# Expert tiles in three groups, half A combined beside the last experts, and one-hot rows made eight choices at a time

## The reference

```python
def _L0_ffn_ref(hidden_states, gate_w, gate_up_proj, down_proj):   # 16 experts, top 2
    logits = x @ gate_w.T
    p = sigmoid(logits); p = p / sum(p)
    w, idx = top_k(p, 2)
    w = w / sum(w)
    gu = einsum('th,ehf->etf', x, gate_up_proj)
    gate, up = split(gu, 2)
    y = einsum('eti,eih->eth', silu(gate) * up, down_proj)
    out = einsum('eth,te->th', y, combine)
x = x + 0.5 * ffn(layernorm(x))
x = x + attn(layernorm(x))          # 16 heads of 16, causal softmax
x = x + 0.5 * ffn(layernorm(x))
```

## Time and profile before

| | us |
|---|---|
| time, median of 3 runs | 887.43 (885.02 to 888.61) |
| profiled execution | 886.32 |
| its span, first to last instruction | 884.6 |
| TensorE busy | 662.1 (75%) |
| VectorE busy | 574.8 (65%) |
| GpSimd busy | 395.4 (45%) |
| ScalarE busy | 366.6 (41%) |
| TensorE's share of the chain that ended last | 64% |

### The profile page before, as it was taken

One profiled execution on the slowest core, in us unless ns is written; L12 is line 12 of the kernel. 1 busy time (PEld: TensorE's weight loads), 2 busy tenths in 40 slices (PEclk: granted clock), 3 DMA queues, 4 the chain that ended last, 5 costly groups with the idle time before them and its releaser, 6 DMA issues.

```text
span 884.6 us, 17856 instructions
## 1 busy us (share of the span) xinstructions
PE 662.1 (75%) x5016; PEld 507.6 (57%) x5017; DVE 574.8 (65%) x1599; ACT 366.6 (41%) x941; POOL 395.4 (45%) x467
## 2 busy tenths in 40 slices
PE   2614999999078999999999999866159999990000
PEld 2402888887056777777777777544038888870000
DVE  6597455555758888878888877646964555553333
ACT  2417334444025555555656655454263333430000
POOL 4101655553453554444555422240026555536775
PEclk9955999999678999999999999988559999995555
DMA  7680455557263444444444433014004555574554
GB/s 238 219 258 10 142 162 162 160 160 137 65 185 106 132 128 120 121 116 129 114 109 121 113 107 97 4 48 144 0 24 142 162 162 161 161 130 130 153 152 142
DMA packets 94136, 113.36 MB, mean 128 GB/s; under 512 B 11633, under 2 KB 84609, under 8 KB 94081
## 3 DMA queue, kind: packets, MB, share of 16 engines
q1 hardware_dynamic: 80224, 74.87, 27.5%
q0 software_dynamic: 13824, 37.77, 17.5%
q10 hardware_dynamic: 32, 0.02, 0.0%
HBM read 49.30 MB, written 33.55 MB: 94 GB/s over the span
## 4 chain that ended last, share of the span: by engine, by line
PE 64%; DVE 12%; DMA 8%; issue 5%; POOL 5%; ACT 4%; SPq 1%; DVEq 0%; ACTq 0%; POOLq 0%
PE bank L774 16%; PE bank L785 8%; PE bank L352 6%; PE bank L411 5%; PE bank L372 5%; PE bank L397 5%; PE bank L767 4%; POOL shared L649 4%; DMA shared<-grouped_out,slot 3%; PE bank L359 3%; PE bank L375 3%; PE bank L431 3%; PE bank L780 2%; DMA normed<-shared 2%; ACT shared L885 1%
## 5 line engine op out<-in xcount | busy, mean ns | idle before, releaser
L632 POOL DMA_INDIRECT shared<-normed,source x160 | 152.3, 952 | 213.4 <-DVE source L1043 111.2
L774 PE MATMUL bank<-wgu_sb,xeT 128*128 x640 | 167.8, 386 | 0.0
L306 POOL TENSOR_SCALAR_AFFINE_SELECT pr<-pr 128x512 f32<-128x512 f32 x128 | 81.0, 655 | 154.8 <-ACT pr L476 154.6
L534 DVE TENSOR_REDUCE mx<-bank 128x2 f32<-128x512 f32 (+1 forms) x192 | 127.0, 685 | 23.6 <-PE bank L375 20.4
L1053 DVE COPY hidT<-bank 128x128 f32<-128x128 f32 x160 | 46.6, 291 | 116.8 <-PE bank L780 115.9
L774 PEld LDWEIGHTS bank<-wgu_sb,xeT 128*128 128x128 f32 x640 | 111.5, 194 | 8.8
L476 ACT ACTIVATE pr<-bank 128x512 f32<-128x512 f32 x192 | 102.9, 609 | 30.6 <-PE bank L397 18.1
L785 PE MATMUL bank<-wd_sb,hidT 128*128 x320 | 95.6, 382 | 0.0
L868 ACT COPY xeT<-bank 128x256 f32<-128x256 f32 x160 | 59.5, 372 | 84.6 <-PE bank L767 84.3
L294 POOL DMA_INDIRECT gathered_rows<-grouped_out,slot x64 | 69.0, 1078 | 27.8 <-DMA grouped_out<-shared 13.4
L872 ACT ACTIVATE silu<-bank 128x128 f32<-128x128 f32 x160 | 44.4, 278 | 83.2 <-PE bank L774 83.2
(11 more groups left out here) (148 smaller groups left out, 1118.2 us busy)
## 6 DMA issues: line engine op xcount, KB each, us to landing
grouped_out<-shared SPq DMA_DIRECT2D x160, 128.0 KB, 1.7
shared<-parts SPq DMA_DIRECT2D x154, 128.0 KB
spare<-parts SPq DMA_DIRECT2D x70, 128.0 KB
normed<-shared SPq DMA_DIRECT2D x16, 512.0 KB, 3.1
x_sb<-in_L_attn_x_dram SPq DMA_DIRECT2D x4, 1024.0 KB, 9.7
wgu_sb<-_L_ffn_gate_up_proj_dram SPq DMA_DIRECT2D x8, 512.0 KB, 8.6
out_dram<-x_sb SPq DMA_DIRECT2D x16, 256.0 KB, 2.6
shared<-normed,source POOLq DMA_INDIRECT x160, 2.8
```

The lines of the kernel that those rows point to most:

```text
L306: nc.gpsimd.affine_select(out=m, in_=m, compare_op=ALU.is_ge, fill=0.0, base=0, pattern=[[0, 4], [1, P]], channel_multiplier=-1).then_inc( ...
L534: nc.vector.tensor_reduce(mx[:, u, h0:h0 + nh], bank[3 + n % 2][:, :].rearrange("p (h k) -> p h k", h=nh), AX.X, ALU.max).then_inc(at["max ...
L632: nc.gpsimd.indirect_dma_start(xe[:, r, :], None, normed, bass.IndirectOffsetOnAxis(source[:, j:j + 1], 0)).then_inc(s["xe_loaded"][r], 16)
L774: last = nc.tensor.matmul(bank[2 + u][:, 0:2 * I], xeT[:, u, c, :], wgu_sb[:, e, c, :], start=(c == 0), stop=(c == HC - 1))
```

## The change

**Expert tiles in three groups.** The 32 token tiles are two halves, A (the first 16) and B. The expert tiles are now laid out as: full tiles that hold only half A's choices (for each expert as many as its count in half A fills), then one tile for each of the 16 experts with the rest of A and the beginning of B, then the rest of B. So all results of half A lie within the first `DONE` = 48 tiles. `ntile`, `end` and `begin` have three parts, and `slot` is computed in more steps.

**Half A combined beside the last experts.** In the second expert stage GpSimd issues 58 fetches, waits until the first 48 tiles are stored, and then takes turns: two result gathers for a token tile of half A, then two fetches, until the fetches are used up. VectorE does twelve combines within the expert rounds, one after every second tile, and the other twenty afterwards. The result buffers are four pairs instead of eight, and the fetched rows have eight buffers in the second stage (`AHEAD`), four in the first.

**One-hots eight at a time.** The rows of eight choices are interleaved, with the choice as the innermost index. VectorE makes them with three operations of 8 x 80, 8 x 128 and 8 x 80 elements on 16-bit data, against two tables that ScalarE fills once per stage. ScalarE's passes in the loop are gone. There are two sets of buffers, and TensorE reads one choice of the eight at a step of eight elements.

**The ones for attention** are written as 32-bit words (half as many elements) in the first expert stage, behind `source`, and attention's VectorE waits ahead of its first step are gone.

```diff
-    LATE = 8
+    EARLY = NT // 2
+    DONE = EARLY * TOPK + E
+    AHEAD = (RING, 2 * RING)
+    LATE = 4
 # GpSimd, second expert stage
-            for j in range(NE_T):
-                fetch(j)
-            for r in range(RING):
-                pool.wait_ge(s["ye_stored"][r], 16 * NK)
-            for t in range(NT):
-                if t >= LATE:
-                    pool.wait_ge(s["x_done"], t - LATE + 1)
+            first_mixed = DONE + AHEAD[f] + 2
+            for j in range(first_mixed):
+                fetch(j)
+            stored_up_to(DONE)
+            for t in range(EARLY):
+                fetch_results(t)
+                for j in range(first_mixed + 2 * t, min(first_mixed + 2 * t + 2, NE_T)):
+                    fetch(j)
+            stored_up_to(NE_T)
+            for t in range(EARLY, NT):
+                fetch_results(t)
 # VectorE, counts
-            link(dve, nc.vector.tensor_tensor(more[:, :, :], cum[:, :, NT - 1:NT].broadcast_to([P, E, NT]),
-                                              thr[:, :].unsqueeze(1).broadcast_to([P, E, NT]), ALU.is_gt))
-            link(dve, nc.vector.tensor_reduce(ntile[:, :], more[:, :, :], AX.X, ALU.add))
+            link(dve, nc.vector.tensor_scalar(tally[:, 1, :], cum[:, :, NT - 1], float(P - 1), None, ALU.add))
+            link(dve, nc.vector.tensor_scalar(tiles_u[:, :, :], tally[:, :, :], shift, None, ALU.logical_shift_right))
...
+            halves = [slice(a * EARLY, (a + 1) * EARLY) for a in range(2)]
+            for a in range(2):
+                link(dve, nc.vector.scalar_tensor_tensor(out=beyond[:, halves[a], :], in0=slot_t[:, halves[a], :], scalar=0.0,
+                                                         in1=jump[:, a, :].unsqueeze(1).broadcast_to([P, EARLY, E]),
+                                                         op0=ALU.is_ge, op1=ALU.mult))
+            for a in range(2):
+                link(dve, nc.vector.tensor_tensor(slot_t[:, halves[a], :], slot_t[:, halves[a], :],
+                                                  base[:, a, :].unsqueeze(1).broadcast_to([P, EARLY, E]), ALU.add))
+            link(dve, nc.vector.tensor_tensor(slot_t[:, :, :], slot_t[:, :, :], beyond[:, :, :], ALU.add))
 # VectorE, one-hots
-                    if j == 0:
-                        nc.vector.tensor_scalar(is_part[:, r, :], lane_h[:, :], part_of[:, t, j:j + 1], None, ALU.is_equal)
-                    nc.vector.tensor_scalar(is_tile[:, r, :], tile_h[:, :], tile_of[:, t, j:j + 1], token[:, bass.ds(t, 1)],
-                                            ALU.is_equal, ALU.mult).then_inc(s["onehot_ready"], 1)
+                nc.vector.tensor_tensor(is_tile[i][:, :, :], tile_rep[:, :, :],
+                                        tile_of[:, rs].unsqueeze(1).broadcast_to([P, NE_T, PLACES]), ALU.is_equal)\
+                    .then_inc(s["match_ready"], 1)
+                nc.vector.tensor_tensor(is_part[i][:, :, :], part_rep[:, :, :],
+                                        part_of[:, rs].unsqueeze(1).broadcast_to([P, P, PLACES]), ALU.is_equal)\
+                    .then_inc(s["match_ready"], 1)
+                dve.wait_ge(s["match_ready"], 2 * k + 2)
+                nc.vector.tensor_tensor(is_tile[i][:, :, :], is_tile[i][:, :, :],
+                                        flat(token_h)[:, rs].unsqueeze(1).broadcast_to([P, NE_T, PLACES]), ALU.mult)\
+                    .then_inc(s["onehot_ready"], 1)
 # TensorE
-                nc.tensor.matmul(bank[5][:, 0:NE_T], is_part[:, r, :], is_tile[:, r, :], start=first, stop=last,
-                                 skip_group_check=True).then_inc(s["source_done"], 1)
+                for r in range(PLACES):
+                    done = nc.tensor.matmul(bank[5][:, 0:NE_T], is_part[i][:, :, r], is_tile[i][:, :, r], start=first and r == 0,
+                                            stop=last and r == PLACES - 1, skip_group_check=True)
 # ScalarE
-                    nc.scalar.activation(distance[:, q, :], lane_h[:, :], ACT.Abs, bias=minus_part[:, bass.ds(k * n + q, 1)])\
-                        .then_inc(s["distance_ready"], 1)
-                    nc.scalar.activation(is_part[:, q * TOPK + 1, :], distance[:, q, :], ACT.Relu, scale=-1.0, bias=one_e[:, 0:1])\
-                        .then_inc(s["second_ready"], 1)
+            nc.scalar.copy(part_rep[:, :, :], lane_h[:, :].unsqueeze(2).broadcast_to([P, P, PLACES])).then_inc(s["rep_ready"], 1)
+            nc.scalar.copy(tile_rep[:, :, :], tile_h[:, :].unsqueeze(2).broadcast_to([P, NE_T, PLACES])).then_inc(s["rep_ready"], 1)
 # VectorE, ones: from the start of attention to behind source in the first expert stage
-            for r in range(RING):
-                dve.wait_ge(ffn[0]["ye_stored"][r], 16 * NK)
-            for i in range(BUFS):
-                last = nc.vector.memset(kT[i][ROWS // 32 * 32:P, :, :], 1.0)
+            if f == 0:
+                dve.wait_ge(s["source_ready"], 1)
+                for i in range(BUFS):
+                    nc.vector.memset(kT_words[i], TWO_ONES).then_inc(at["ones_set"], 1)
 # VectorE, second expert stage
+            def mixed_round(i):
+                for r in range(0, 2 * RING, 2):
+                    expert_round(i * 2 + (alone + r // RING), range(r % RING, r % RING + 2))
+                    combine(r // 2, i * LATE + r // 2, i)
```

242 lines of the change are left out of this document (134 added, 108 removed).

## The result

The changed kernel takes 857.29 us (median of 4 runs, 854.66 to 858.55) beside 887.96 of the kernel before: ratio 0.966, interval 0.9625 to 0.9689. A second group of runs gave 856.33 (854.44 to 857.61) beside 886.44: 0.966, 0.9637 to 0.968. So it is 30 us faster where 38 were predicted, inside the range (844 to 869), just above the forecast's own range (844 to 856), and no rival's case.

What follows compares the result with a forecast made beforehand. GpSimd's issue rate was taken to bound the 80 us tail; choice stretches and attention's memsets could also give time. Span 884.6 - 22.7 - 9.3 - 6.1 = 846.5, plus 2.8 to the runs' median: 849 us, range 844 to 869.

Steps and rivals of the forecast that it cites:

- forecast's own range: Whole kernel without the rivals: 844 to 856 us, allowing for the gathers' pace, the count chains and a warmer TensorE.
- Part 3: One-hots in both routing stages: rounds of 1.54 us, 14.5 us in sum, so 7.3 and 7.6 us less.
- part 2: Counts on VectorE, in both routing stages: a longer chain of operations, 2.8 us more each, 2.3 to 3.5.
- The two rivals on the choices: One-hot loops: TensorE paces them (15 in 100), or VectorE is no faster an element (8 in 100); either way 869 us.
- Part 1: Last expert stage and tail: result gathers start earlier, 86 GpSimd issues at 1.263 us set the end, 22.7 us less.
- +5.3: Last stage: upper bound if the 44 issues beside busy engines take 1078 ns instead of 958, 5.3 us worse.
- The margin of 3 us: End of the experts: last stores there at about 813, GpSimd asks after 54 issues at 815.7, so it never waits.
- Part 4: Start of attention: memsets no longer stand ahead of the first combine, 6.1 us less, 5 to 6.3.
- only shifts: Attention behind the first combine: a chain through VectorE, ScalarE and stacking DMAs keeps its length and starts earlier.
- the third that I had forecast: Mixed turns of the last stage: TensorE idles a third of each, needing 3.25 us where GpSimd needs 5.05.
- Lockstep: Mixed turns: gathers wait for combines, combines for expert rounds, rounds for fetches; 77 us more, 927; 2 in 100.

Runs made afterwards that it cites:

- after again: Second profile of the unchanged changed kernel, span 855.1 us; its group of runs took 856.33 us beside 886.44 of the kernel before.
- one-hots-alone kernel: The kernel before with only the eight-at-a-time one-hots added, its counts, last stage and memsets as before: 875.38 us, 0.9879 of before.
- the 20 buffers: The changed kernel with 20 input buffers instead of 8 in the second expert stage: 845.77 us, 0.9538 of before.

## Why the prediction was right, and where 8 us went

- **Part 3 and part 2** held at their places: -15.7 for -14.9, +6.1 for +5.6, rounds of 1.51 to 1.58 after the first for 1.54. The two rivals on the choices are refuted by the row of 8 matmuls in 1.38 us and by the 0.49 and 0.68 of the operations. Part 2 says that five operations go and then sums nine; nine is right.
- **Part 1** held in its mechanism: the first result gather came 90.1 us after the first fetch (90.2), 86 issues set the end, the order is worth 21.9. The term gave 19.1 instead of 22.7, since the 86 issues took 4.2 us more than their sum (mean of two profiles). I bounded the pace by busy engines during the first 44 issues, and by +5.3; those 44 lost only 0.8 and 0.5. About 2 are the two pauses behind the last stores and about 1 the long issues of the last 30 gathers (mean 0.99 to 1.00 instead of 0.96), both behind those 44. The combine had also changed its form, to a loop with an address register, and I had priced that at nothing.
- **The margin of 3 us** at the 55th issue was spent: in after again the last fetch landed in 4.47 us instead of 2.74, and the gather behind the last store came 10.4 us after the last transposes instead of 8.1. Of these 2.3 us the store itself is 1.4 (3.10 instead of 1.70); a combine of VectorE (799.43 to 800.5) stands in the same chain, ahead of a late tile's copy of its hidden rows. I used transfers from a quiet queue for a queue with two streams in it.
- **Part 4** was 6.1 and is 5.3: the root of the variance stands behind GpSimd's eighth gather. The step "only shifts" failed, because with the memsets gone another engine's order was late next. The memsets were covered as foreseen.
- **"What is behind it only shifts"** failed a second time, by more: attention's body took 3.3 us more. The one-hots-alone kernel shows 2.3 of it with the attention's program untouched, so neither the memsets' move nor the counts are needed for it. The cause stays open; the long issue of a stacking transfer is 0.6 to 1.6 us over the others, and no run shows how much of it reaches the end.
- **TensorE in the mixed turns** idled 20% of 735 to 770 us and 32% of 770 to 805 in after again, at a granted clock of 1.00, near the third that I had forecast once the look-ahead of eight tiles was used up. In the other profile it idled 16 and 22% at a clock of 0.94 and 0.92: fewer idle us because the same work ran more slowly, not because there was more of it. Neither mattered: GpSimd's issues set the pace, as the 20 buffers show, which took 12 of them away from that stretch and gained 10.6 us.
- **Lockstep,** the rival with 2 in 100, was right to leave out of the sum on chips where before takes 886 us. On the two slower chips its wait appears in every profile of the mixed order, with 20 to 23 us. The order has little in reserve, and its gain on a slower chip is not known, since the changed kernel itself never ran there.

## What to carry to other kernels

When one engine's issue count is the bound of a tail, count what it still has to issue from the moment the data are there, and move every issue that can go ahead of it: deeper input buffers gave 10.6 us on top of the reordering's 21.9, for two lines. Where engines wait for each other in a ring, ask what one stall does to it: here, on two chips, stalls of some us were followed by about 20 us of waits for combines. Price a moved loop in its new form and beside its new neighbours; the durations of a quiet stretch (landing 2.74, issue 0.96) are a lower bound there. And when a stall of 12 us goes, look in each engine's own order for what it had hidden, here a root behind eight gathers.

## What the runs showed that I had not expected

- Two-source operations on 16-bit operands from SBUF, one of them repeated by a step of zero, cost VectorE 0.51 ns for each further element; the f32 forms here cost 1.065.
- A matmul whose weights and rows lie 16 bytes apart, element by element, is as fast as a dense one at the lower clock level to 0.01 us: 8 in 1.38 us, 7 dense ones in 1.15. At the full level nothing here shows it.
- Setting 32 x 2048 words of f32 takes 1.76 us, and such memsets start 2.14 us apart; 32 x 4096 elements of bf16, the same bytes, take 3.47 and start 4.28 apart.
- Kernel and chip may interact: on two chips the kernel before loses 9 to 10 us (896 and 895 for 886), and the new order with written-out combines takes 31 to 42 us more than its like without them on the others. Some 20 of these are GpSimd's waits for combines, which come behind shorter stalls whose cause no profile names.
